# Loading the normalisation rows and W2 inside the edge stage, and eight two-step ScalarE writes for the selection matrices, in a graph network kernel

## The reference, cut to what matters

```
# layer 0: message passing, GRU, batch norm
m    = relu(concat(h[src], edge_attr) @ W1.T + b1) @ W2.T + b2
agg  = segment_sum(m, dst)
gi, gh = agg @ W_ih.T + b_ih, h @ W_hh.T + b_hh        # -> r, z, n gates
h_new = (1 - z) * n + z * h
bn   = gamma * (h_new - run_mean) * rsqrt(run_var + eps) + beta
x    = layernorm(x + h + bn)
# layer 1: two relational layers
w    = einsum('rb,bio->rio', att, basis)               # 30 bases, 2 relations
msg  = gate_r(x_j) * x_j @ w[r];  agg = segment_sum(msg, row)
out  = agg + x @ root + bias
x    = layernorm(x + out)
```

## Time and profile before

| what | us |
|---|---|
| runs | 514.34, 510.9, 512.93 (median 512.93) |
| the profiled execution | 510.66 |
| its span, first to last instruction | 508.9 |
| TensorE busy | 483.9 (95%) |
| VectorE busy | 293.1 (58%) |
| ScalarE busy | 194.3 (38%) |
| GpSimd busy | 100.3 (20%) |

### The profile page before, as it was taken

One profiled execution on the slowest core, in us unless ns is written; L12 is line 12 of the kernel. 1 busy time (PEld: TensorE's weight loads), 2 busy tenths in 40 slices (PEclk: granted clock), 3 DMA queues, 4 the chain that ended last, 5 costly groups with the idle time before them and its releaser, 6 DMA issues.

```text
span 508.9 us, 6645 instructions
## 1 busy us (share of the span) xinstructions
PE 483.9 (95%) x2231; PEld 299.2 (59%) x2231; DVE 293.1 (58%) x568; ACT 194.3 (38%) x347; POOL 100.3 (20%) x115
## 2 busy tenths in 40 slices
PE   7999969999999998999999999998899999999995
PEld 2434325545554555866765666574666677787774
DVE  5886659899889899275012579766213115441323
ACT  1887674443344444273035022674232013232000
POOL 0000626677666620000000230000000150000000
PEclk9999979999999999999999999999999999999998
DMA  8959886778778745959787798678997350200011
GB/s 251 428 215 364 326 299 194 252 252 273 235 244 262 244 161 232 408 217 352 319 338 287 291 326 296 256 296 331 401 381 291 151 161 1 82 1 1 21 43 43
DMA packets 29206, 121.20 MB, mean 238 GB/s; under 512 B 4282, under 2 KB 7306, under 8 KB 24686
## 3 DMA queue, kind: packets, MB, share of 16 engines
q1 hardware_dynamic: 17518, 92.33, 47.4%
q0 software_dynamic: 7856, 24.91, 16.0%
q10 hardware_dynamic: 3792, 3.43, 2.2%
HBM read 113.85 MB, written 6.82 MB: 237 GB/s over the span
## 4 chain that ended last, share of the span: by engine, by line
PE 83%; DVE 5%; DMA 5%; ACT 2%; issue 2%; DVEq 1%; another core or an unknown queue 1%; SPq 0%
PE ps L1400 17%; PE ps L1340 16%; PE ps L1235 13%; PE ps L1200 9%; PE ps L1438 9%; PE ps L1281 5%; DMA basis<-in_basis 5%; PE ps L1282 4%; PE ps L1379 3%; PE ps L1167 3%; ACT CT L628 2%; PE ps L1225 1%; PE ps L1178 1%; PE ps L1414 1%
## 5 line engine op out<-in xcount | busy, mean ns | idle before, releaser
L1235 PE MATMUL ps<-X 128*128 128x512 f32 x158 | 74.5, 612 | 0.0
L655 ACT ACTIVATE rhi<-x 128x512 fp32r<-128x512 f32 x79 | 47.2, 631 | 70.6 <-DVE x L927 47.6
L1200 PE MATMUL ps<-basis,sel 128*32 128x512 f32 x496 | 58.7, 596 | 4.6 <-DMA basis<-in_basis 3.2
L595 POOL DMA_DIRECT2D X<-w_layer x32 | 16.9, 653 | 214.4 <-DMA w_layer<-ev 214.4
L586 POOL DMA_INDIRECT X<-u_rows,esrc x40 | 42.4, 1061 | 80.3 <-DMA u_rows<-X 52.9
L934 DVE SCALAR_TENSOR_TENSOR rlo<-x,rhi 128x512 fp32r<-128x512 f32 x79 | 50.7, 684 | 2.1 <-ACT rhi L655 2.1
L1438 PE MATMUL ps<-Xr,CT_r 128*128 128x512 f32 x200 | 47.0, 389 | 0.0
L1235 PEld LDWEIGHTS ps<-X 128*128 128x128 f32 x158 | 29.2, 196 | 28.6 <-issue 28.4
L586 POOL DMA_INDIRECT x_sb<-u_rows,esrc x39 | 40.8, 1045 | 18.8 <-DVE x L927 9.8
L1438 PEld LDWEIGHTS ps<-Xr,CT_r 128*128 128x128 f32 x200 | 37.5, 188 | 7.8
L1073 DVE SCALAR_TENSOR_TENSOR Xr<-ps,gate,Xr 128x512 fp32r<-128x512 f32 x20 | 14.9, 750 | 43.5 <-ACT Xr L743 43.5
(11 more groups left out here) (211 smaller groups left out, 749.4 us busy)
## 6 DMA issues: line engine op xcount, KB each, us to landing
basis<-in_basis SPq DMA_DIRECT2D x29, 2048.0 KB
X<-in_eaT SPq DMA_DIRECT2D x20, 256.0 KB
basis<-in_basis SPq DMA_DIRECT2D x8, 512.0 KB
X<-w_layer POOLq DMA_DIRECT2D x32, 128.0 KB, 3.0
w_layer<-ev SPq DMA_DIRECT2D x13, 256.0 KB, 10.5
X<-in_WhhT SPq DMA_DIRECT2D x3, 1024.0 KB, 13.6
basis_apart<-in_basis SPq DMA_DIRECT2D x1, 2048.0 KB, 19.4
X<-in_WihT SPq DMA_DIRECT2D x2, 1024.0 KB, 10.3
```

Of the source, the lines that this page charges most:

```text
L655: nc.scalar.activation(rhi[:, u % 2, s], pre[:, s], ACT.Relu).then_inc(hi_ready, 1)
L1200: mm = pe.matmul(bank[32 * g:32 * g + 32], sel[:, layer, s], held[:, g, s2], start=(s == 0), stop=(s == 3), tile_position=(0, 32 * g))
L1235: pe.matmul(ps[:, EA_BANKS[s]], eaT[:, u % 2, s * P:(s + 1) * P], W1bT, start=True, stop=True).then_inc(ea_done, 1)
```

## The change

Two edits. First, the waits and loads of L511 to L514 move into the loop of `load_attributes`, behind iteration 1, whose second half can start only when unit 1's attributes are computed. Second, two writes of `sel` that differ only in s (columns 16r + s and every second one after them, in neighbouring blocks of 32) become one write of 128x2x8: the two rows start 33 columns apart, so a view of 66 columns with rows of 33 describes both, and `sel` becomes one flat tile with 18 spare columns at its end so that the last view stays inside. The values and places written are the same.

```
-        sel = sb("sel", [P, 2, 4, 32])
+        sel = sb("sel", [P, 2 * 4 * 32 + 18])
...
+        def both_rows(layer, group, r):
+
+            at = 128 * layer + 64 * group + 16 * r
+            return sel[:, at:at + 66].rearrange("p (s c) -> p s c", c=33)[:, :, 0:2 * BLK:2]
...
             for c in range(APART + 1, EARLY * SLOTS):
                 load_basis(sp, c)
-            sp.wait_ge(basis_used, APART // 2 + 1)
-            for i, a in enumerate(t["bn"]):
-                sp.dma_start(bn_rows[:, i], a.broadcast_to([P, H])).then_inc(const_in, 16)
-            sp.dma_start(W2T[:], t["W2T"]).then_inc(w2_in, 16)
-
             assert SLOTS == 2
             plain = UNITS // 2 - SLOTS * 4
             for it in range(1, plain):
                 load_attributes(it)
+                if it == 1:
+                    sp.wait_ge(basis_used, APART // 2 + 1)
+                    for i, a in enumerate(t["bn"]):
+                        sp.dma_start(bn_rows[:, i], a.broadcast_to([P, H])).then_inc(const_in, 16)
+                    sp.dma_start(W2T[:], t["W2T"]).then_inc(w2_in, 16)
...
                             for group in range(2):
-                                for s in range(2):
-                                    last = nc.scalar.activation(
-                                        sel[:, layer, 2 * group + s, 16 * r + s:16 * r + 16:2], maskc[:], ACT.Copy,
-                                        scale=att[:, group, layer, r:r + 1])
+                                last = nc.scalar.activation(
+                                    both_rows(layer, group, r), maskc.rearrange("p (s c) -> p s c", s=1
+                                                                               ).broadcast_to([P, 2, BLK]),
+                                    ACT.Copy, scale=att[:, group, layer, r:r + 1])
...
-                            mm = pe.matmul(bank[32 * g:32 * g + 32], sel[:, layer, s],
+                            mm = pe.matmul(bank[32 * g:32 * g + 32], sel[:, 128 * layer + 32 * s:128 * layer + 32 * s + 32],
```

## The result

| | before | after |
|---|---|---|
| runs, us | 510.54 to 514.59 (6), median 513.27 | 517.24 to 520.73 (6), median 519.19 |
| the profiled execution | 510.66 | 518.33 |
| its span | 508.9 | 516.5 |
| mean granted clock | 0.991 | 0.984 |

The change makes the kernel slower: 1.0127 times the time before, 95% interval 1.0093 to 1.0162. The median lies outside the predicted range of 509.0 to 517.6 us.

The account below looks back on a forecast made before the run. TensorE, busy 95% of the span, was taken to bound the kernel. ScalarE 0, the stretch at 65 us 0 and the wait at 92.8 us +1.0 gave 513.9 us on the median's scale (512.93 before), range 509.0 to 517.6.

Parts of the forecast that it names:

- ScalarE: Writes of `sel` from 23.66 us: eight for sixteen gain 1.6 us on ScalarE, hidden by 31 us, so 0 on the path.
- the lower bound: Time of one new 128x2x8 write on ScalarE: at least 0.198 us, as for a write of half the elements.
- The stretch at 65 us: SyncE's queue without the five loads: less DMA traffic, but nothing on the path waits for it, so gain 0.
- the transition loosens: Rival, near 60 to 71 us: removing the loads returns 3.2 us of late release and 3.4 of half clock; 506.3 us, chance 0.12.
- The issues: SyncE's queue: the five loads issue from 81.7 to 83.9 us, in time for the next attribute load at 87.27.
- The landing: Iteration 2's first attribute load lands at 93.6 us against TensorE's need at 92.80, a wait taken as 1.0 us.
- The sum: Landing estimate: W2T issued about 83.5 us, landing 9.4 us later at 92.9, then 0.7 us for the attribute load: 93.6.
- the 6.45 us of the sum: Time of all sixteen DMA engines for the five loads: 7.16 us less 0.71 for one attribute load.
- The upper end of 3.3 us: Longest wait for the attribute load near 92.8 us, if gathers take half of the engines all the time; landing at 96.1.
- the rule: Each DMA engine takes one packet from each queue in turn; gathers under way keep turns, giving a 3.3 us wait, not 1.0.
- that wait and the clock: Rival: the wait at 92.8 us lasts 3.3 us and halves the clock, costing 3.4 more; 519.6 us, chance 0.09.
- It needs the worst landing: Argument against the slower rival: its 3.3 us wait requires the attribute load to land at the latest time considered, 96.1 us.

Follow-up runs that it names:

- the writes alone: Kernel before with only the eight two-step writes of `sel`, the five loads left in the count stage: 507.94 against 508.4 us, ratio 0.9997.
- The kernel with the loads spread: Changed kernel with the same 2 MB in eight pieces of 256 KB, one behind each of iterations 1 to 8: 509.8 against 508.64 us, ratio 1.0031.
- the set with 508.4 us: Runs in which the kernel before took 508.4 us; beside it, the eight writes by themselves took 507.94 us and the five moved loads by themselves 515.4 us.
- the loads alone: Kernel before with the five loads moved behind iteration 1 and the sixteen writes kept: 515.4 against 508.4 us, ratio 1.0134.
- the quarters: Changed kernel with W2T as four loads of 256 KB at iteration 1, the four rows back in the count stage: 509.38 against 509.1 us, ratio 1.0008.

## Why the prediction was wrong, point by point

**ScalarE: right.** Eight writes for sixteen, seven of them in 1.49 us, so 0.21 us each from start to start, next to the lower bound. The gain of some 1.5 us is hidden as said; the writes alone changed nothing (0.9997).

**The stretch at 65 us: right.** Less DMA, the same length, the same 3.6 us idle and a fallen clock. The kernel with the loads spread frees this stretch and has no wait for an attribute load elsewhere, and it gained nothing. The rival *the transition loosens* is out: the 3.2 us release of the earlier trace rows is at 59.87 us again, 3.23 long, with the five loads gone from this place. In the set with 508.4 us it is absent from the traces of the writes alone and of the loads alone, one with the loads at the old place and one at the new, so it does not hang on them.

**The issues: right.** Gamma issued at 81.75 (said 81.7), the attribute load at 87.27 as before.

**The landing: this is the step that failed.** The mechanism was right: one wait at that place, for that load. The term that was mis-sized is the landing of the attribute load, and with it the wait, 1.0 us said and 5.1 measured. The sum said that W2T lands 9.4 us after its issue, since that was so for the same loads before, and the attribute load 0.7 us behind it: 93.6. It landed at 98.02. Where W2T's landing can be read (the loads alone), it took 12.5 us, 3.1 more, and the attribute load came 2.1 us behind it (83.83 + 10.99 against an issue at 80.24 + 12.5) and not 0.7, 1.4 more: 4.5 us together, where the error is 4.4. The engines' time that the bulk loads need was not far off. From 82 to 93.3 us the queues show (packets, MB, share of 16 engines):

```profile
q1 hardware_dynamic: 876, 2.31, 56.2%
q0 software_dynamic: 349, 1.16, 28.0%
```

56.2% of 11.3 us are 6.35 us. That includes iteration 1's second attribute load, which the sum put at 0.7 us, and leaves out the end of W2T, for the 6.45 us of the sum. What was wrong is that this time would be had as quickly as in the quieter place: 28.0% went to gathers, and 16% of those 11.3 us stayed empty, 1.8 us, most of it while transfers were waiting. The upper end of 3.3 us took an equal share with the gathers, with the engines always at work, for the worst case; it had no term for engines that stand idle.

**Why the landing time held in the count stage and not here:** shown is that the form of the four rows matters, and only in a crowd. By themselves the four single-row broadcasts cost 2.3 us of waiting, and the same bytes packed cost none; in the change, packing them fills the engines and brings the wait to 0.7 and 0.5 us in two traces. A part is plain issue time: the four issues put W2T 2.27 us behind iteration 1's second attribute load (81.38 to 83.65), the packed one 0.85 us (80.78 to 81.63), so its head start over iteration 2's load is 3.6 us for 5.0. A part is engine time: 1.0 us more for the rows than for the quarters beside gathers, and none alone. It stays open why the four rows leave engines unused beside gathers. No run tells it, and the other order, W2T ahead of the rows, was not run.

By the Trainium skill (DMA: Bandwidth & Descriptors, section on queues, rings and completion order) each engine goes round its queues, one packet from each. This case's traces bear that out in part. Here gathers kept 28.0% of the engines beside the bulk loads, and in a queue of its own the attribute load gained 0.7 to 1.3 us. Against it stands, with 1.1% from 66 to 72 us: in the changed kernel the same three gathers, with the five loads gone, take 30.3% there, so in the kernel before the bulk loads did hold them back. As a price the rule does not do: it gave 3.3 us of waiting, and 5.1 were measured.

**The rival that came true** is *that wait and the clock*, chance 0.09: one wait, at 92.8, the clock behind it. It said 3.3 + 3.4 = 6.7 us and 519.6; it was 5.1 + 2.7 = 7.8 us in the trace, and the median is 5.9 us above before. That 519.6 stands so near to the measured 519.19 is luck, since the wait was priced too low and the clock too high. Of the 6.8 us at half clock that the rival counted, 2.1 us lay in the idle stretch itself, where they cost nothing: 4.71 / 2 = 2.4 us would have been its price. Its condition, an idle stretch over 2.6 to 3.6 us, was met. "It needs the worst landing" was wrong reasoning: the landing was beyond what I had called the worst. The chance was too low because a single landing, taken with fewer gathers beside it, was carried into a stretch that the earlier trace rows showed at 72% of the engines.

## What to carry to other kernels

A transfer that nobody waits for can still make the next one in its path late: before moving bulk loads, look for the transfer with the least slack behind them, and compare the traffic of both places. A landing time holds for the traffic that was beside it: the 9.4 us of W2T became 12.5 in a busier place. Here several broadcasts of single rows were better laid side by side and loaded as one, and the 2 MB of bulk loads cost least in that busy stage in pieces between the loads that are needed soon.

## What the runs showed of the hardware that was not expected

- **The same idle time does not always drop the clock.** Ahead of the transition's zero matmuls TensorE stood still for 3.39 us in the kernel with the writes alone, and its clock was 0.65 from 68 to 72 us; with W2T in quarters it stood still for 3.38 us, and the clock stayed at 1.00:

```profile
68.00:72.00 4.00, 2.84 (x6) 1.53 (x8) 0.69 (x1) 2.42 (x6) 0.39 (x1) 0.65 1.03 413
```

```profile
68.00:72.00 4.00, 2.90 (x9) 1.55 (x11) 1.67 (x3) 2.61 (x7) 0.26 (x2) 1.00 0.95 372
```

  So the point from which a wait costs clock is not one length. Of seven traces that stood still for 3.38 or 3.39 us there, three kept 1.00 and four had half clock behind it. At the wait for a part of `basis` late in the kernel, an idle stretch of 2.59 us had half clock behind it in the kernel with the loads alone (it began at 357.8 us; clock 0.72 from 360 to 364 us), where the kernel before kept 1.00 after 2.64 us.

- **A write of two stepped rows of eight costs little more than a write of one.** 128x2x8 took 0.21 us from start to start, 128x8 0.198.
